# Keeping v and its convolution in DRAM as bands of eight rows, in a one-core attention and mixture-of-experts kernel

## What is computed

```python
xn  = layernorm_over_channels(layernorm_over_channels(x)) * ln_w + ln_b
qkv = conv3x3_depthwise(w_qkv @ xn)              # 576 channels, zero padding
q, k, v = split(qkv) ; each * spatial_interaction
attn = softmax(temperature * normalise(q) @ normalise(k).T)   # per head, 24 x 24, over all pixels
x = x + w_proj @ (attn @ v)
t = tokens(x)                                    # 16384 tokens of 192
probs = softmax(layernorm(t) @ gate_w + gate_b)  # 4 experts, the top 2 kept and rescaled
t = t + sum_e probs_e * (gelu(layernorm(t) @ w1_e + b1_e) @ w2_e + b2_e)
```

## Time and profile before

| | |
|---|---|
| time, median of 3 runs (lowest to highest) | 2177.44 us (2176.84 to 2178.6) |
| the profiled execution: its time, its span | 2176.08 us, 2174.3 us |
| TensorE matmul busy, granted clock | 1884.7 us, 0.951 |
| VectorE, ScalarE, GpSimd busy | 1508.9, 1224.0, 1235.5 us |
| DMA, mean | 165 GB/s, 359.04 MB in 307268 packets |

### The profile page before, as it was taken

One profiled execution on the slowest core, in us unless ns is written; L12 is line 12 of the kernel. 1 busy time (PEld: TensorE's weight loads), 2 busy tenths in 40 slices (PEclk: granted clock), 3 DMA queues, 4 the chain that ended last, 5 costly groups with the idle time before them and its releaser, 6 DMA issues.

```text
span 2174.3 us, 35768 instructions
## 1 busy us (share of the span) xinstructions
PE 1884.7 (87%) x9782; PEld 1514.5 (70%) x9782; DVE 1508.9 (69%) x3488; ACT 1224.0 (56%) x2355; POOL 1235.5 (57%) x1122
## 2 busy tenths in 40 slices
PE   5688888888867468775899999999999999999966
PEld 3456555555544345555799898888989888888854
DVE  4799999999968663455666767667676765556533
ACT  3465656566645233323666666666666767667632
POOL 3666666666666540035866766766667677444330
PEclk9899999999989788987999999999999999999988
DMA  5342222222223257777788788888888787676659
GB/s 130 91 124 68 80 79 61 73 80 73 64 68 103 61 139 211 203 205 234 226 211 225 217 223 220 219 226 215 224 225 218 195 248 202 168 182 167 158 135 351
DMA packets 307268, 359.04 MB, mean 165 GB/s; under 512 B 26536, under 2 KB 256680, under 8 KB 307112
## 3 DMA queue, kind: packets, MB, share of 16 engines
q1 hardware_dynamic: 251624, 288.22, 45.1%
q0 software_dynamic: 50880, 60.59, 14.0%
q10 hardware_dynamic: 4608, 8.39, 1.0%
HBM read 222.76 MB, written 134.35 MB: 164 GB/s over the span
## 4 chain that ended last, share of the span: by engine, by line
PE 49%; DMA 6%; DVE 3%; POOL 3%; issue 3%; ACT 2%; SPq 1%; POOLq 0%; DVEq 0%; ACTq 0%
PE bank L1772 20%; PE bank L1788 13%; PE bank L1789 6%; PE bank L1755 3%; PE bank L1815 3%; DMA yo<-v_scratch 3%; DMA xn<-acc_scratch 2%; PE bank L1807 2%; POOL xs_scratch L1233 1%; POOL acc_scratch L1248 1%; DMA acc_scratch<-yo,tix 0%; PE bank L1837 0%; ACT yo L1289 0%; DVE b2w L983 0%; ACT x_all L1284 0%
## 5 line engine op out<-in xcount | busy, mean ns | idle before, releaser
L1248 POOL DMA_INDIRECT acc_scratch<-yo,tix x268 | 439.5, 1640 | 303.1 <-DVE yo L1627 241.1
L1772 PE MATMUL bank<-x_all,w1b 128*128 128x512 f32 x2010 | 549.4, 403 | 1.0 <-ACT hf L1299 1.0
L1788 PE MATMUL bank<-w_hl,hh 128*128 x1608 | 495.6, 360 | 7.1 <-DVE hl L1726 6.1
L1299 ACT ACTIVATE hf<-bank,b_col 128x512 f32<-128x512 f32 x402 | 277.1, 689 | 335.1 <-PE bank L1772 335.0
L1726 DVE TENSOR_TENSOR hl<-hf,hh 128x512 fp32r<-128x512 f32 x402 | 277.1, 690 | 271.1 <-ACT hh L1302 270.7
L1789 PE MATMUL bank<-w_hl,hl 128*128 x1608 | 404.7, 252 | 0.0
L595 DVE SCALAR_TENSOR_TENSOR acc<-zwin,wdw,acc 128x512 f32<-128x512 f32 (+2 forms) x462 | 401.2, 908 | 2.6
L1772 PEld LDWEIGHTS bank<-x_all,w1b 128*128 128x128 f32 x2010 | 348.5, 189 | 55.4 <-ACT hf L1299 1.4
L1788 PEld LDWEIGHTS bank<-w_hl,hh 128*128 128x128 f32 x1608 | 301.9, 188 | 41.9 <-issue 11.2
L1789 PEld LDWEIGHTS bank<-w_hl,hl 128*128 128x128 f32 x1608 | 305.9, 190 | 17.4
L1233 POOL DMA_INDIRECT xs_scratch<-xn,idx x256 | 262.1, 1024 | 85.0 <-issue 75.0
(11 more groups left out here) (256 smaller groups left out, 3049.8 us busy)
## 6 DMA issues: line engine op xcount, KB each, us to landing
w1b<-w1s_scratch SPq DMA_DIRECT2D x134, 768.0 KB, 4.9
xs<-xs_scratch SPq DMA_DIRECT2D x67, 522.0 KB, 6.1
yo<-v_scratch SPq DMA_DIRECT2D x64, 240.0 KB, 3.9
xtok_scratch<-xtok SPq DMA_DIRECT2D x32, 384.0 KB, 2.6
v_scratch<-zv SPq DMA_DIRECT2D x64, 192.0 KB
vc_scratch<-yo SPq DMA_DIRECT2D x64, 192.0 KB, 3.0
vd<-vc_scratch SPq DMA_DIRECT2D x64, 192.0 KB
xtok<-xtok_scratch SPq DMA_DIRECT2D x32, 384.0 KB, 6.8
```

Of the source, the lines that this page charges most:

```text
L1248: nc.gpsimd.indirect_dma_start(acc_dram, bass.IndirectOffsetOnAxis(ap=tix[:, J % 4, t:t + 1], axis=0), yo[:, J % YN, t, :], None, compute_ ...
L1299: nc.scalar.activation(hf[:, k % 3, :], lb[k % 2][:, :], ACT.Gelu, bias=b1_col[:, bass.ds(exp_of[J] * CH + k, 1)]).then_inc(gelu, 1)
L1772: last = nc.tensor.matmul(lb[k % 2][:, :], w[:, q, :], v[:, J % 2, :], start=(i == 0), stop=(i == 4))
L1788: nc.tensor.matmul(yb[t][:, 0:2 * C], hh[:, k % 3, cols], w, start=(k == 0), stop=False, skip_group_check=True)
```

## The change

- `v_scratch` is laid out as (half, 10 rows of a band, channel, 16 bands, 128): the four bands of a unit now lie together, 2 KB for each partition, 64 KB from one partition's piece to the next. The first and last rows of each band are also held by the neighbour, so a step of phase 1 has, except at the two ends, two more stores of 96 by 512 B.
- `vc_scratch` is laid out as (half, row of a band, channel, band, 128). A unit is stored in pieces of 2 KB. A step of the projection is now four rows that lie eight apart, so its loads of the convolved v are pieces of 2 KB; x, the sum and the token numbers follow by strided slices.
- `zr` has six buffers (`NZ`) and no padding columns (these are in the split buffers, set once); loads run five ahead (`AHEAD`). The store of a unit is issued by ScalarE right after its eviction.
- The weights of all 16 bands are made at once as a table of 120 by 384 elements, split into a high and a low table; a band matrix is then two products on VectorE of a table with a mask. GpSimd builds no bands; ScalarE no longer rounds them.

```diff
-        v_dram = nc.dram_tensor("v_scratch", (2, H + 2, G2, W), FP32, kind="Internal").ap()
-        vc_dram = nc.dram_tensor("vc_scratch", (2, H, G2, W), FP32, kind="Internal").ap()
+        NV = H // RV
+        v_dram = nc.dram_tensor("v_scratch", (2, RV + 2, G2, NV, W), FP32, kind="Internal").ap()
+        vc_dram = nc.dram_tensor("vc_scratch", (2, RV, G2, NV, W), FP32, kind="Internal").ap()
...
                         sp.wait_ge(z_a, 5 * i.val + 5)
+                        r0 = 1 + ROWS * i.par
+                        edge, beside = (0, RV + 1), (0, i.half - 1)
+                        if i.par:
+                            edge, beside = (ROWS - 1, 0), (0, i.half + 1)
                         for g in (0, 1):
-                            sp.dma_start(v_view[:, g, bass.ds(i.val * ROWS + 1, ROWS), :],
+                            sp.dma_start(v_dram[g, r0:r0 + ROWS, :, bass.ds(i.half, 1), :].rearrange("r p a w -> p r (a w)"),
                                          zv[0:G2, g, :].rearrange("p (r w) -> p r w", w=W)).then_inc(st_v, 16)
+                            if i.within(1, NB - 2):
+                                sp.dma_start(v_dram[g, edge[1], :, bass.ds(beside[1], 1), :].rearrange("p a w -> p (a w)"),
+                                             zv[0:G2, g, edge[0] * W:edge[0] * W + W]).then_inc(st_v, 16)
...
-                            wait(act, st_v, 48 * i.val)
+                            wait(act, st_v, 80 * i.val - 32)
...
+        def row(s, t):
+            return Q_STEPS * (ROWS * (s // Q_STEPS) + t) + s % Q_STEPS
...
                 def load_unit(u):
-                    wait(sp, zl_ok, u - 2)
-                    sp.dma_start(zr[:, u % 3, :, 1:W + 1], bands).then_inc(ld_z[u % 3], 16)
+                    wait(sp, zl_ok, u - NZ + 1)    
+                    sp.dma_start(zr[u % NZ], rows[:, 4 * s:4 * s + 4, :]).then_inc(ld_z[u % NZ], 16)
-                def store_unit(u):
...
-                    sp.wait_ge(cv_a, u + 1)
...
-                    sp.dma_start(rows[r0:r0 + 4 * MV, :].rearrange("(b p) w -> p b w", p=MV),
-                                 cv[:, u % 2, :].rearrange("p (b w) -> p b w", w=W)).then_inc(st_c[u % 2], 16)
...
                 for u in range(BANDS):
-                    load_unit(u + 3)
-                    store_unit(u)
+                    load_unit(u + AHEAD)
...
                 def evict(u):
                     act.wait_ge(cv_t, u + 1)
                     wait(act, st_c[u % 2], 16 * (u // 2))
                     nc.scalar.activation(cv[:, u % 2, :], cb[u % 4][0:MV, :], ACT.Copy).then_inc(cv_a, 1)
+                    act.wait_ge(cv_a, u + 1)
+                    act.dma_start(rows[:, 4 * s:4 * s + 4, :], cv[:, u % 2, :].rearrange("p (b w) -> p b w", w=W)).then_inc(st_c[u % 2], 16)
...
+                def band(q):
+                    for piece, out in ((taps, b_hi[q]), (taps_lo, b_lo[q])):
+                        last = nc.vector.tensor_tensor(out.rearrange("p k (r c) -> p k r c", c=CV),
+                                                       piece[:, q, :, :, None].to_broadcast([KV, 3, RV, CV]),
+                                                       same_ch[:, None, None, :].to_broadcast([KV, 3, RV, CV]), ALU.mult)
+                    last.then_inc(bl_ok, 1)
...
+                nc.vector.reduce_sum(same_ch, ident[0:KV, 0:KV].rearrange("p (r c) -> p c r", c=CV), AX)
+                for ky in range(3):
+                    last = nc.vector.reduce_sum(row_of[:, ky, :], ident[0:KV, CV * ky:CV * ky + MV].rearrange("p (r c) -> p r c", c=CV), AX)
...
+                w9 = wcol.rearrange("p h g k -> p (h g) k")
+                for ky in range(3):
+                    nc.vector.tensor_tensor(term if ky else taps, w9[:, :, 3 * ky:3 * ky + 3, None].to_broadcast([KV, BANDS, 3, RV]),
+                                            row_of[:, ky, None, None, :].to_broadcast([KV, BANDS, 3, RV]), ALU.mult).then_inc(tp_l, 1)
+                    if ky:
+                        dve.wait_ge(tp_l, 1 + 2 * ky)
+                        nc.vector.tensor_tensor(taps, taps, term, ALU.add).then_inc(tp_l if ky == 1 else tp_ok, 1)
...
+                dve.wait_ge(th_ok, 1)
+                nc.vector.tensor_tensor(taps_lo, taps, taps_hi.bitcast(FP32), ALU.subtract).then_inc(tp_ok, 1)
...
                 for u in range(BANDS):
-                    if u % 2 and u + 2 < BANDS:
-                        band_of(nc.vector, u + 2, bl_d)
                     if u + 2 < BANDS:
-                        band_lo(u + 2)
+                        band(u + 2)
                     z_rest(u + 2)
```

More of the change, by code:

```diff
@@ L860, in build, with rows_of @@
         assert u0 == UNITS and len(units_at[n_a - 1]) <= len(units_at[0])
+        def row(s, t):
+            return Q_STEPS * (ROWS * (s // Q_STEPS) + t) + s % Q_STEPS
+        def rows_of(s, first=0, count=ROWS):
+            return slice(row(s, first), row(s, first + count - 1) + 1, Q_STEPS)
+        assert Q_STEPS == RV
         def unit(u):
@@ L949, in build @@
             BW = 3 * MV
-            zr = window(yo, 0, KV, 3, 4, W + 2)
-            cv = window(yo, 3 * ZW, MV, 2, 512)
+            NZ, AHEAD = 6, 5
+            cv = window(yo, 0, MV, 2, 512)
+            zr = [window(yo, 1024 + 512 * n, KV, 4, W) for n in range(4)] + [window(hf, 512 * n, KV, 4, W) for n in range(NZ - 4)]
             z_hi = [window(x_all, n * ZW, KV, 4, W + 2) for n in range(3)]
@@ L956, in build @@
             b_lo = [window(t, o, KV, 3, MV) for t, o in band_place[BANDS:2 * BANDS]]
-            bsum = window(b2w, 0, KV, 2, 3, MV)
-            bterm = window(b2w, 2 * BW, KV, 2, 3, MV)
-            band = window(b2w, 4 * BW, KV, 3, MV)
+            BT = BANDS * 3 * RV
+            taps, term, taps_lo = (window(b2w, n * BT, KV, BANDS, 3, RV) for n in range(3))
+            taps_hi = window(hl, 3 * BW, KV, BANDS, 3, RV)
+            same_ch = window(b2w, 3 * BT, KV, CV)
+            row_of = window(b2w, 3 * BT + CV, KV, 3, RV)
             attn = window(xs, 0, G2, 4, 2 * G2).rearrange("p k (g c) -> p k g c", g=2)
@@ L966, in build @@
             at_v, at_t, at_a, at_p = sem("at_v"), sem("at_t"), sem("at_a"), sem("at_p")
-            ld_wc, bc, bl_p, bl_d, bh_ok, bl_ok = (sem(n) for n in ("ld_wc", "bc", "bl_p", "bl_d", "bh_ok", "bl_ok"))
-            bs_ok = [sem(f"bs_ok{n}") for n in range(2)]
-            ld_z = [sem(f"ld_z{n}") for n in range(3)]
+            ld_wc, zp_ok, tp_l, tp_ok, th_ok, bl_ok = (sem(n) for n in ("ld_wc", "zp_ok", "tp_l", "tp_ok", "th_ok", "bl_ok"))
+            ld_z = [sem(f"ld_z{n}") for n in range(NZ)]
             st_c = [sem(f"st_c{n}") for n in range(2)]
             zh_ok, zl_ok, cv_t, cv_a = (sem(n) for n in ("zh_ok", "zl_ok", "cv_t", "cv_a"))
[L973 to L987, removed]
             c2, ld_g = sem("c2"), sem("ld_g")
@@ L1044, in load_unit @@
                     q, s, h, g = unit(u)
[L1045 to L1058 removed]
+                    rows = v_dram[h].rearrange("r (c g) b w -> g (r c) b w", g=GV)[g]
+                    wait(sp, zl_ok, u - NZ + 1)
+                    sp.dma_start(zr[u % NZ], rows[:, 4 * s:4 * s + 4, :]).then_inc(ld_z[u % NZ], 16)
                 def load_prep(s):
@@ L1126, in _ @@
                     sp.dma_start(wcol[r * CV:r * CV + CV, :, :, :].rearrange("p h g k -> p h (g k)"), taps).then_inc(ld_wc, 16)
-                sp.wait_ge(bc, 1)
-                for u in range(3):
+                for u in range(AHEAD):
                     load_unit(u)
@@ L1195, in _ @@
                 nc.gpsimd.tensor_tensor(n2[:, 2, :], n2[:, 0, :], n2[:, 1, :], ALU.pow).then_inc(at_p, 1)
-                for q in range(2, BANDS, 2):
-                    band_of(nc.gpsimd, q, bl_p)
                 nc.gpsimd.memset(zrow[:, :, :], 0.0).then_inc(c2, 1)
```

81 lines of the change are left out of this document (33 added, 48 removed).

## The result

| | before | changed |
|---|---|---|
| median of 4 runs | 2177.97 us | 2110.74 us (2107.51 to 2112.59) |
| profiled execution, its span | 2176.08, 2174.3 us | 2107.51, 2105.4 us |
| ratio | | 0.9691, 95% interval 0.9678 to 0.9703 |

The forecast was 2109.5 us. The profiled execution is 68.6 us shorter than that of before, against 67.6 in the forecast. Run once more, in five rounds beside three of its variants, the changed kernel took 2109.84 us.

The account below looks back on a forecast made before the run. PE fills the blocks, so the place to look was 722 to 1006 us, held by bands, v loads and scatters. Terms 30.1 + 24 + 6.5 + 7 = 67.6, say 68, gave 2108.1, median 2109.5 us; 8 in 10: 2095 to 2136.

Parts of the forecast that it names:

- The first 16 units: Units 0 to 15, before the beats: PE sets the pace instead of the bands, ending at 774.2, 30.1 us earlier.
- Beats 0 to 6: From unit 15's end to the end of the prefix sums: 97 us against 121.1, 24 us earlier.
- Loads and stores: A unit's load lands in 3 us (bounds 2.6 and 9.4), covered by about 11 us with five in flight.
- A load now waits only for the rest of unit u-1: In SyncE's list, once stores leave it: a load's only wait is for that rest, done two units earlier.
- the circle: ScalarE stood 78.7 us for loads of v, SyncE 76.8 for evictions; loads queued behind stores; moving the stores opens it.
- a load still ends idle time at ScalarE: Sign that the prediction is wrong: ScalarE's wait for v's load was to be near nothing.
- more than 1 us a beat at the eviction: Sign that the prediction is wrong: in the beats, eviction waits on the store by more than this.
- rival 1: Beats stay with the stores, evictions waiting on late ones: 2147 us, or 2125 at a landing of 5 us; chance 0.15.
- rival 2: More than forecast: no dip, no late store, zeros hidden, VectorE never late: 82 us less, 2096; chance 0.07.
- From the prefix sums to the scatter: From beat 6's prefix sums to the first scatter: 13.2 us instead of 19.7, 6.5 us earlier.
- The scatters: GpSimd's scatters wait less for VectorE's moments: 7 us earlier (bounds 3 and 10).
- Rivals 3, 4 and 5: Phase 1 gives back up to 25 us (0.06); 64 KB pitch slows it (0.03); stretch doesn't bind, about 2177 (0.03).

Follow-up runs that it names:

- the kernel with the third buffer: The changed kernel with three instead of two `cv` buffers for the convolved unit that ScalarE evicts and stores: 2100.13 us, ratio 0.9651.
- the changed kernel three deep: The changed kernel with v units loaded three deep (three buffers, three ahead) instead of six buffers and five ahead: 2118.50 us, ratio 0.9747.
- the kernel beside it: The changed kernel with each edge store that phase 1 adds issued once more to a spare tensor: 2110.39 us, ratio 0.9702.

## Why the forecast was right, and where it was not

**The first 16 units and the beats: the sum right, the border between them misread.** The forecast put the end of unit 15 before at 804.28, the end of a row of 18 matmuls. It is the end of unit 18. The timeline of PE in the kernel before has the last matmul on unit 15's low band here, with one of its own left, the first of the second row:

```profile
796.71 0.40 PE L1755 MATMUL bank<-x_all 120*96 120x512 f32 x1
796.94 2.53 PE L1755 MATMUL bank<-x_all,w1b 120*96 120x512 f32 x10
```

Its windows to either side of that (columns as in the earlier trace rows) count 155 matmuls up to 797.3, 144 of them (9 x 16) of the 16 units, 10 of the attention, and the first of unit 16:

```profile
736.60:797.30 60.70, 43.69 (x155) 27.89 (x156) 49.09 (x78) 22.14 (x50) 37.69 (x55) 0.88 0.39 106
797.30:871.00 73.70, 58.10 (x225) 40.52 (x224) 22.91 (x65) 21.74 (x40) 2.46 (x4) 0.86 0.74 205
```

So the term *The first 16 units* was worth 60.6 - 39.8 = 20.8 and 2.3 for the start, 23.1 us, not 30.1. The term *Beats 0 to 6* was 128.1 - 96.2 = 31.9, not 24. Together 55.0 against 54.1. The three units of beat 0 were booked to the wrong term, and the sum can't see that. The experiments can: taking the tables away costs 25.3 us, not 30. That the total came out within 1.3 us is for this part luck of bookkeeping: what one term had too much the next had too little.

**The new durations held.** Unit 0 at 734.44 (forecast 735.4), 39.8 us for 16 units (38.8), unit 15 at 774.2 (774.2). The product of a band is the group `w1b<-b2w` of 120x288, 21 of them at 450 ns (0.47 taken from the earlier trace rows). A unit takes 2.12 us on TensorE (2.2).

**The beats, 96.2 us (97).** Right in sum, with the reserve differently spent. TensorE's own count is 88.4 us: 32 units of 2.12, seven projections of 2.72, the prefix sums at 0.63 and 0.9 of waiting for the mask; at 2.2 a unit the forecast counted 91.0. The 3 us for stores of zeros and the 3 for dips and late stores came to 7.8: four stalls, 5.2 us in all, and most of the rest a lower clock right behind them (the unit after the largest takes 3.87 us instead of 2.12). One stall, 1.11 us, follows the late load of unit 23. The largest, 2.25, falls where the four stores of zeros, issued from 810.5 to 814.9 us, have filled DMA (windows of the changed kernel, columns as in the earlier trace rows):

```profile
814.00:822.00 8.00, 8.00 (x39) 6.20 (x38) 3.90 (x16) 3.27 (x7) 1.22 (x2) 1.00 1.02 365
822.00:830.00 8.00, 5.75 (x22) 3.45 (x22) 2.63 (x7) 3.18 (x6) 0.00 (x0) 0.92 1.01 306
```

So the zeros may be in that late store; no run moves them, and it is not shown. The second profile of the changed kernel has 93.6 us for the beats, so such a term of one execution is good to 2 or 3 us, and a hit within 1 us is in part luck. The mean granted clock is 0.98 in the beats, against 0.86 before, when TensorE kept starting and stopping.

**Loads and stores.** The load of v was taken at 3 us and measured 6.0, at most 11.6, above the bound of 9.4. The row it came from, x in phase 1, had the same pitch and pieces, but a DMA share of 0.28 around it (100 to 700 us, before) and not 0.85. The 11 us of cover saved the sum. *A load now waits only for the rest of unit u-1* failed once, at the wait for the 16 stores in SyncE's list, 8.4 us: the same pattern as the circle, left in by the change. In the kernel with the third buffer the one stall of TensorE left in the beats, 1.86 us, again follows the load of unit 23; no run takes the wait away, so its price is not shown. With it came the prediction's sign that a load still ends idle time at ScalarE, three times, 5.1 us in all. *The circle above is opened* by the move of the stores, the forecast said; the runs show that either the move or the depth opens it, and that the second adds 8 to 12 us to the first, not another 28.

**The store wait.** The prediction gave a sign of being wrong: more than 1 us a beat at the eviction. It was 41.0 us in all, and it cost 9 to 10 us. That is rival 1's mechanism, at its mild end (it gave 16 us at a landing of 5, the median was 3.7). It was underpriced because only the pace of evictions was counted, not the split queued behind a waiting one. Without it the kernel takes 2100 us, close to rival 2's 2096, which had no late store.

**From the prefix sums to the scatter**: 870.37 to 883.59, 13.2 us as forecast. **The scatters**: 945.13 to 1006.33 before, 883.59 to 938.98 after, 61.2 - 55.4 = 5.8 us (7); of the two waits left, the one of 3.09 us goes back along the chain to the late stores near 891 and 900 us. The rest to the end: 1167.97 before, 1166.42 after, 1.6 us less (0 forecast); in the second profile of the changed kernel it is 1169.8, so the 1.6 us can't be told from nothing. The blocks keep their length, 1082.9 us before and 1082.1 after from the first turning to the last product. The terms then read 23.1 + 31.9 + 6.5 + 5.8 + 1.6 = 68.9, the difference of the spans.

**Rivals 3, 4 and 5** fell: phase 1 pays nothing, also with its edge stores doubled; loads land at most 11.6 us after issue and overlap, and the old layout is no faster; the stretch does set the end.

How much each part gave depends on the order in which they are put in. From before to the changed kernel one path is, by the ratios: stores moved, 29 us; deep loads and layout on top (the changed kernel with old bands), 12; tables, 25. Another: tables, 20; stores moved and layout (the changed kernel three deep), 36; deep loads, 10 to 12 (8 by the kernel beside it). What isn't shown: deep loads alone in the kernel before.

## What to carry to other kernels

A wait in a DMA-issuing list holds everything queued behind it: look for two engines that each stand about as long for the other, and open the circle by another list or by more depth, but count it once. When a duration is taken from a transfer that ran in a quiet stretch, check it against the number that will be in flight, and ask what stands behind each wait in an in-order list, not only how often it comes round or how long it is in sum. And mark the border between two terms by something countable, nine matmuls a unit here; a chain row's end is not a unit's end.

## What the hardware showed that was not expected

- The number in flight did more to the landing of a load than the size of its pieces. Pieces of 2 KB landed in 6.0 us up to five deep and in 4.4 us three deep. At five deep, pieces of 512 B landed in 6.3 us and stores in 4.1 instead of 3.7. In the kernel before, three deep, 512 B pieces landed in 3.9 us.
- Pieces of 2 KB took less DMA for the same bytes: a share of 0.85 at 265 GB/s in the beats, against 0.96 at 260 GB/s with pieces of 512 B. The time differs by about 3 us, at the edge of what the runs resolve.
- TensorE's mean granted clock was higher where it was fed without gaps: 0.86 from 797 to 871 us before, 0.98 from 774 to 871 us after.
